# Filter pass: the column components' differences and low halves issued by GpSimd instead of VectorE

## What is computed

```python
def _conv_att2(x, kg_w1, kg_b1, kg_w2, kg_b2, lk_filter, fus_w, fus_b):
    f_att, f_idt = (x[:, :ATT], x[:, ATT:])
    ...
    ker = (hdn @ kg_w2.T + kg_b2).reshape(b, ATT, 1, SK, SK)
    ...
    out_lk = _conv(f_att, lk_filter, pad=LK // 2)
    out = jnp.concatenate([out_lk + out_dk, f_idt], axis=1)
    return _conv1x1(out, fus_w, fus_b)
...
out = att(feats[0])
for i in range(1, LEVELS):
    k = 2 ** i
    out = out + jnp.repeat(jnp.repeat(att(feats[i]), k, axis=2), k, axis=3)
return _conv1x1(out, fin_w, fin_b)
```

## Time and profile before

| what | value |
|---|---|
| median of 3 runs | 2874.56 us (2873.55 to 2876.15) |
| the profiled execution | 2871.94 us |
| its span | 2870.1 us |
| TensorE busy, whole span | 2608.4 us (91%) |
| VectorE busy, whole span | 2145.4 us (75%) |
| ScalarE busy, whole span | 1055.7 us (37%) |
| GpSimd busy, whole span | 643.5 us (22%) |

### The profile page before, as it was taken

How to read it: one execution, slowest core, us unless ns; L and a number is a source line. 1 busy time by engine, 2 the same in 40 slices (tenths; PEclk the granted TensorE clock), 3 DMA queues, 4 the chain that set the end, 5 groups by cost and what they waited for, 6 DMA issues and landing times. The chain is left out here.

```text
span 2870.1 us, 38870 instructions
## 1 busy us (share of the span) xinstructions
PE 2608.4 (91%) x12262; PEld 2086.3 (73%) x12262; DVE 2145.4 (75%) x2968; ACT 1055.7 (37%) x1641; POOL 643.5 (22%) x663
## 2 busy tenths in 40 slices
PE   5999999979998799999998788888947999999998
PEld 4777777757887688888886566666735777777776
DVE  5444444554454788888887889999878999999998
ACT  1211111111100688989987322222103333333332
POOL 6544444312220534444443100000001000000000
PEclk9999999978887899999999799999968999999999
DMA  8222222210000877777775234334442333333332
GB/s 149 69 75 76 75 77 74 54 34 6 13 13 15 192 218 222 217 219 219 219 215 165 78 119 150 135 135 150 157 172 97 102 117 92 102 115 93 100 119 59
DMA packets 288702, 338.04 MB, mean 118 GB/s; under 512 B 24816, under 2 KB 243824, under 8 KB 274288
## 3 DMA queue, kind: packets, MB, share of 16 engines
q1 hardware_dynamic: 280736, 334.74, 39.4%
q10 hardware_dynamic: 7888, 2.29, 0.5%
HBM read 211.60 MB, written 122.62 MB: 116 GB/s over the span
## 5 line engine op out<-in xcount | busy, mean ns | idle before, releaser
L168 PE MATMUL ps_all<-vh,u_h 128*128 128x512 f32 x960 | 384.6, 401 | 29.6 <-DVE vl L2825 28.8
L170 PE MATMUL ps_all<-vh,u_l 128*128 128x512 f32 x960 | 383.1, 399 | 0.0
L169 PE MATMUL ps_all<-vl,u_h 128*128 128x512 f32 x960 | 382.6, 399 | 0.0
L2734 ACT ACTIVATE vh<-rt,gn 128x528 fp32r<-128x528 f32 x192 | 130.4, 727 | 446.2 <-DVE rt L2802 320.5
L168 PE MATMUL ps_all<-vh,t_h 128*128 128x512 f32 x576 | 231.1, 401 | 23.7 <-DVE vl L1874 23.7
L168 PEld LDWEIGHTS ps_all<-vh,u_h 128*128 128x128 f32 x960 | 180.7, 188 | 83.3 <-issue 36.9
L169 PE MATMUL ps_all<-vl,t_h 128*128 128x512 f32 x576 | 230.0, 399 | 0.0
L170 PE MATMUL ps_all<-vh,t_l 128*128 128x512 f32 x576 | 229.1, 398 | 0.0
L170 PEld LDWEIGHTS ps_all<-vh,u_l 128*128 128x128 f32 x960 | 180.9, 188 | 46.1
L169 PEld LDWEIGHTS ps_all<-vl,u_h 128*128 128x128 f32 x960 | 181.0, 189 | 45.4
L1713 POOL TENSOR_TENSOR zr<-zr,z 128x256 f32<-128x256 f32 x128 | 124.5, 993 | 340.0 <-DMA xr<-in_x 340.0
(11 more groups left out here) (407 smaller groups left out, 6627.2 us busy)
## 6 DMA issues: line engine op xcount, KB each, us to landing
xr<-in_x SPq DMA_DIRECT2D x128, 256.0 KB, 3.5
x_layer<-xr SPq DMA_DIRECT2D x64, 512.0 KB, 2.7
xq<-x_layer SPq DMA_DIRECT2D x32, 1024.0 KB, 4.8
x_layer<-xq SPq DMA_DIRECT2D x32, 1024.0 KB, 3.8
out<-ot SPq DMA_DIRECT2D x64, 512.0 KB, 5.2
xw<-in_x SPq DMA_DIRECT2D x112, 288.0 KB, 4.3
xc<-in_x SPq DMA_DIRECT2D x120, 256.0 KB, 3.9
xw<-x_layer SPq DMA_DIRECT2D x16, 1152.0 KB, 8.7
```

The lines of the kernel that those rows point to most:

```text
L168: pe.matmul(o, wh, xh, start=first, stop=False, skip_group_check=True)
L169: pe.matmul(o, wh, xl, start=False, stop=False, skip_group_check=True)
L170: return pe.matmul(o, wl, xh, start=False, stop=last, skip_group_check=True)
L2734: act.activation(vh[:, v % 2, n, :, :].rearrange("p a b -> p (a b)"), rt[:, n, :, :].rearrange("p a b -> p (a b)"), ACT.Identity, scale=gn ...
```

## The change

`raw`, `differences` and `low` move word for word from VectorE's block into GpSimd's (only the engine's name differs), and GpSimd gets a `period` of its own that issues them in the order of the components. In VectorE's `period` all calls of the three are taken out; the order of what is left there is unchanged. ScalarE, TensorE and SyncE keep their orders and waits. GpSimd now also waits at its start for the filter's weights (`b_s`) and for the cleared margins (`b_p`), since `ea`, `eb` and `rw` hold weights before.

```diff
+                    def raw(n, k):
...
+                        pool.tensor_tensor(rw[:, k % 3 - 1, :, :], v[0], v[1], ALU.subtract).then_inc(r_d, 1)
...
+                    def differences(n, first):
...
+                        pool.tensor_tensor(ea[:, :, :, :], fx[:, 0:2, :, :], fx[:, 2:4, :, :], ALU.subtract).then_inc(e_d, 1)
+                        pool.tensor_tensor(eb[:, :, :, :], fx[:, 2:4, :, 0:8], fx[:, 0:2, :, 1:9],
+                                          ALU.subtract).then_inc(e_d, 1)
...
+                    def low(n, k):
...
+                        pool.tensor_tensor(cl[:, k, :, :], src, ch[:, k, :, :].bitcast(F32), ALU.subtract).then_inc(v_l, 1)
+
+                    def period(i, a, s, n):
+                        if i is not None:
+                            raw(i, 8)
+                            low(i, 8)
+                        if n is not None:
+                            raw(n, 1)
+                            low(n, 0)
+                            raw(n, 2)
+                            low(n, 1)
+                            low(n, 2)
+                            differences(n, i is None)
+                            raw(n, 4)
+                            low(n, 3)
+                            raw(n, 5)
+                            low(n, 4)
+                            low(n, 5)
+                            raw(n, 7)
+                            low(n, 6)
+                            low(n, 7)
+
+                    b_s.at(pool, 0, NBS)
+                    pool.wait_ge(b_p, 4)
+                    schedule(pool, period)
...
                 @block.vector
                 def _(dve):
-                    def raw(n, k):
...
-                    def differences(n, first):
...
-                    def low(n, k):
...
                     def period(i, a, s, n):
                         first = i is None
-                        if i is not None:
-                            raw(i, 8)
                         if a is not None:
                             outputs(a, 2)
-                        if i is not None:
-                            low(i, 8)
...
                         if n is not None:
-                            raw(n, 2)
                             dynamic_sums(n, 0, first)
                         if s is not None:
                             variance(s)
                         if n is not None:
-                            low(n, 2)
                             low_dynamic(n, 0)
...
```

More of the change, by code:

```diff
@@ L2148, in _ @@
                     assert b_g.n == NBG
+                    def raw(n, k):
+                        m = 6 * n + 2 * (k // 3) + k % 3
+                        if not (isinstance(m, int) and m < 3):
+                            pool.wait_ge(v_l, 9 * n + (k - 2 if k > 2 else 0))
+                        if k == 1:
+                            pool.wait_ge(xp_f, 16 * (n + 1))
+                        v = {1: (fx[:, 2, :, 0:8], fx[:, 3, :, 0:8]), 2: (fx[:, 3, :, 0:8], fx[:, 0, :, 1:9]),
+                             4: (ea[:, 0, :, 0:8], ea[:, 1, :, 0:8]), 5: (ea[:, 1, :, 0:8], eb[:, 0, :, :]),
+                             7: (eb[:, 0, :, :], eb[:, 1, :, :]), 8: (eb[:, 1, :, :], ea[:, 0, :, 1:9])}[k]
+                        if k > 3:
+                            pool.wait_ge(e_d, 2 * n + 2)
+                        pool.tensor_tensor(rw[:, k % 3 - 1, :, :], v[0], v[1], ALU.subtract).then_inc(r_d, 1)
@@ new lines, in differences @@
+                    def differences(n, first):
+                        if not first:
+                            pool.wait_ge(v_l, 9 * n)
+                        pool.wait_ge(xp_f, 16 * (n + 1))
+                        pool.tensor_tensor(ea[:, :, :, :], fx[:, 0:2, :, :], fx[:, 2:4, :, :], ALU.subtract).then_inc(e_d, 1)
+                        pool.tensor_tensor(eb[:, :, :, :], fx[:, 2:4, :, 0:8], fx[:, 0:2, :, 1:9],
+                                          ALU.subtract).then_inc(e_d, 1)
@@ new lines, in low @@
+                    def low(n, k):
+                        src = rw[:, k % 3 - 1, :, :] if k % 3 else (fx[:, 3, :, 0:8], ea[:, 1, :, 0:8], eb[:, 1, :, :])[k // 3]
+                        pool.wait_ge(v_h, 9 * n + k + 1)
+                        if k % 3:
+                            pool.wait_ge(r_d, 6 * n + 2 * (k // 3) + k % 3)
+                        elif k:
+                            pool.wait_ge(e_d, 2 * n + 2)
+                        else:
+                            pool.wait_ge(xp_f, 16 * (n + 1))
+                        pool.tensor_tensor(cl[:, k, :, :], src, ch[:, k, :, :].bitcast(F32), ALU.subtract).then_inc(v_l, 1)
@@ L2431, in period @@
                         if n is not None:
-                            raw(n, 1)
                             dynamic_taps(n, first)
-                            low(n, 1)
                         if s is not None:
@@ L2452, in period @@
                             low_lk(a, 1)
[L2453 to L2456, removed]
                         if a is not None:
                             add_attention(a, 1)
-                        if n is not None:
-                            low(n, 4)
                         if a is not None:
                             low_lk(a, 2)
-                        if n is not None:
-                            raw(n, 5)
                         if s is not None:
@@ L2478, in period @@
                         if n is not None:
-                            raw(n, 7)
                             dynamic_sums(n, 2, first)
@@ L2483, in period @@
                         if n is not None:
-                            low(n, 7)
                             low_dynamic(n, 2)
```

4 lines of the change are left out of this document (removed).

## The result

Before 2874.8 us, after 2924.65 us (medians of 4 runs each, 2873.55 to 2876.15 and 2923.7 to 2925.49): ratio 1.0174, 95% interval 1.0160 to 1.0189. The change costs 50 us. The profiled execution of after took 2925.49 us (span 2923.7, before 2870.1), its mean granted clock was 0.925 (before 0.936).

A forecast was written before the change was run, and what follows sets the result against it. VectorE, busy 61.1 of 64.7 us per filter-pass period, was fullest, all three TensorE waits being for its order. Six periods (5 x 5.7 + 2.2 = +30.7) and the start (+5.3) gave +36: 2910 us said, range 2862 to 2940.

The forecast's parts named there:

- A0 and A1: Starts of attention of quarters 0 and 1 in a filter-pass period; the stretch between was forecast at 24.8 instead of 15.6 us.
- The port taken in turns: After component 2, GpSimd and VectorE alternate whole instructions; third dynf ends at 8.9 us, w_l starts at 10.5.
- the border steps: ms, colf and two rowf on VectorE beside GpSimd's second run wait a turn each, costing 3.5 us more.
- the rival without them: Only two-input operations are held, not ms, colf, rowf: +2.2 us per period, 2893 us; 12%.
- Prices on GpSimd: GpSimd operations: 1.3 us for 560 elements, 2.75 and 2.55 for the 1260 and 1120 elements; 26.5 us per period.
- A1 to the next A0: Rest of the period, from attention of quarter 1 to the next attention of quarter 0: 45.6 instead of 49.2 us, -3.6.
- the wait I myself forecast at 14 us: TensorE's wait for the low half ll ahead of A1, near 14 us instead of 4.6.
- no slow clock: TensorE from A1 to the next A0 without any wait or slow clock would need 43.3 us.
- The sum: Five periods at +5.7, the first at +2.2, the start at +5.3: in all +36 us.
- The first period: First of six periods with both attention and a next image; no border steps, so 3.5 us less: +2.2.
- The start: GpSimd alone carries image 0, delaying ScalarE's copy cc for component 3: 32.4 instead of 27.1 us, +5.3.
- The rival that the gain comes through: GpSimd holds VectorE little: A0 to A1 14.9, period 58.6 us, -6.1 each, start +4, total 2842; 18%.

The follow-up runs named there:

- The kernel with the filled wait: Changed kernel plus 55 dummy products on TensorE (36 in the period without the filter of s) covering its wait before attention 1: 2894.9 us, ratio 1.0071.
- the run that undoes it: Changed kernel with image 0's low halves and differences made by VectorE in the old order, GpSimd starting with image 1: 2909.1 us, ratio 1.0126.
- the same work does at other places: Changed kernel with all moved work still on GpSimd, its runs placed beside the quarters' sums: 2852.0 us, ratio 0.9930.
- The 2841 us with image 0 on VectorE: Changed kernel with GpSimd's runs beside the quarters' sums and image 0's chain on VectorE in the old order: 2841.1 us, ratio 0.9883.
- the kernel with image 0 on VectorE: Changed kernel with only image 0's chain back on VectorE, GpSimd's runs otherwise not moved: 2909.1 us, ratio 1.0126.
- 44 dummy products: Changed kernel plus 44 matmuls of 128x512 with unused results on TensorE, directly ahead of attention 1: 2917.6 us, ratio 1.0151.
- the last run: Kernel with runs beside the quarters and image 0 on VectorE, with GpSimd's component 7 and raw component 8 moved behind VectorE's outputs: 2858.5 us, ratio 0.9951.

## Why the prediction was right, and where its sum was not

The direction was right, and so was the mechanism between A0 and A1. The time is 15 us above the forecast and inside the range, but two errors went against each other, and that is luck: the five periods are 22 us longer behind A1 than the sum had it, and 6 us shorter between A0 and A1. By the steps:

- *The port taken in turns.* Right. The third `dynf` was expected to end 8.9 us after component 2 and did so after 8.6; `w_l` 10.5 and 10.0; the first add 16.8 and 15.55. The difference is mostly the border steps: 2.7 us more than before instead of 3.5. They are held, which no row of before showed for instructions as short and for which the section of the Trainium skill named there gives the rule; the rival without them is out. A0 to A1: 24.8 forecast, 23.54 measured, so +8.0 instead of +9.2.
- *Prices on GpSimd.* 1.3 us for 560 elements: 1.29 undisturbed (1827.56 in after), 1.61 on average for the 48 low halves, with turns lost to VectorE. The pair took 3.21 and 2.56 instead of 2.75 and 2.55 beside VectorE.
- *A1 to the next A0: the term that failed.* The sum took TensorE at full clock there. It was "45.6 instead of 49.2, -3.6", and came out at 51.24, +2.1. The chain itself was rather too long than too short: with TensorE's clock kept up it is 43.8 to 45.8 us, against the 45.6 of the sum. What I left out is that the wait I myself forecast at 14 us would be followed by TensorE at half clock, 14.10 against 19.84 us up to attention 2. I had even written "with no slow clock" beside the 43.3 us and put no price on the other case. The rows of before had one: A1 there begins at 0.80 us instead of 0.51, after a wait of 4.63.
- *The sum.* Five periods: 46 forecast between A0 and A1 and 39.8 measured; -18 forecast behind A1 and +4.3 measured. The kernel with the filled wait lies 21 us above the kernel before; by this difference the other 29 of after's 50 us are clock.
- *The first period*: +2.2 forecast, +0.4 measured. *The start*: +5.3 forecast, +6.3 measured, and 6.7 by the run that undoes it.
- *The rival that the gain comes through*, with A1 14.9 us behind A0, a period of 58.6 and 2842 us, is what the same work does at other places: 14.9, 58.5 to 61.3, and 2852. The 2841 us with image 0 on VectorE meet the rival's 2842 in part by chance, since the rival had 4 us for the start, which that run takes away, and its periods are shorter than most of that run's. The rival was wrong for this change because both engines' runs start from the same event.

Open is why the clock comes back 3 to 5 us behind A1 in some periods and after some 13 in others of the same kernel with the same wait; these two cases differ by some 5 to 6 us a period. In after and in the kernel with image 0 on VectorE it goes with the place at which the clock falls in the wait. With 44 dummy products it does not: there it fell 2.1 to 2.2 us into the wait and came back 3.1 us behind A1 once and 12.8 to 13.2 three times, and once it did not fall at all. No run here sets which one it is. The pair's price apart from the place of what follows it was not separated either.

## What to carry to other kernels

Before work goes to GpSimd, mark each VectorE instruction as held (two inputs in SBUF, fp32 copy or `tensor_scalar`) or free (an input in PSUM, statistics), short ones too, and place GpSimd's reads beside the free ones: the same work was 1.7% slower or 0.7% faster by place alone, and 1.2% faster with the first image's left on VectorE. A wait that grows on TensorE can have a second price behind it, its clock; it counts only where TensorE is late there, and filling the wait with dummy products tells whether it is. When one engine's piece is delayed, look at what every other engine has queued behind the wait for it.

## What the runs showed of the hardware beyond what was expected

- A copy of 64x128 waits for a whole GpSimd instruction like a long one: 2.83 us for 0.22, one of 128x32 1.40 for 0.20.
- `memset` on GpSimd of 1260 and 1120 elements (1.14 and 1.02 us) holds no `dynf` of VectorE; no copy or `tensor_scalar` on SBUF stood beside it.
- The length of a stand does not tell what it costs. One of 2.6 to 2.9 us (44 dummy products) cost as much as one of 12.6 in three periods of five: 19.8 to 20.0 us from A1 to attention 2, against 14.1 without a stand. One of 2.65 us in the last run (A1 at 1871.85) cost nothing: 14.10 us, clock 1.00.
- After waits of 4.5 to 4.7 us the kernel before was back at full clock 3.2 to 3.8 us behind A1 in all five periods.
